# Four transformer blocks on one core: rows kept in expert order across two stages, raw context rows mixed ahead of their projection, rotation ahead of scaling

## What is computed

```
L0: m = memory @ W_mem.T                       # context projected to 256
    a = softmax(x @ m.T / 16);  c = a @ m
    x = rmsnorm(x + sigmoid([x, c] @ W_gate.T + b) * c)
L1, L3: vm = expert mask of the token          # two weight sets, v and l
    q, k, v = rope(where(vm, n(x) @ v_qkv, n(x) @ l_qkv))
    x += where(vm, ctx @ v_dense, ctx @ l_dense)      # causal self attention, 16 heads of 16
    x += cross_attention(n(x), context)               # 16 heads of 8
    x += where(vm, v_ffn(n(x)), l_ffn(n(x)))          # silu(gate) * up, 688 wide
L2: x += tanh(g) * latent_attention(layernorm(x), context)   # 16 heads of 64
    x += tanh(f) * gelu_ffn(layernorm(x))
```

## Time and profile before

| | us |
|---|---|
| median of 3 runs | 2231.86 |
| the profiled execution, its own time | 2225.6 |
| its span (first to last instruction) | 2223.8 |
| PE busy | 2066.6 (93%) |
| DVE busy | 1368.3 (62%) |
| ACT busy | 1139.9 (51%) |
| POOL busy | 853.1 (38%) |
| mean granted TensorE clock | 0.967 of full |

### The profile page before, as it was taken

One profiled execution on the slowest core, in us unless ns is written; L12 is line 12 of the kernel. 1 busy time (PEld: TensorE's weight loads), 2 busy tenths in 40 slices (PEclk: granted clock), 3 DMA queues, 4 the chain that ended last, 5 costly groups with the idle time before them and its releaser, 6 DMA issues.

```text
span 2223.8 us, 62412 instructions
## 1 busy us (share of the span) xinstructions
PE 2066.6 (93%) x23424; PEld 1669.0 (75%) x23425; DVE 1368.3 (62%) x2791; ACT 1139.9 (51%) x2603; POOL 853.1 (38%) x1109
## 2 busy tenths in 40 slices
PE   7988898879979998999999979999999979979998
PEld 5656676656659997788888868897777756659997
DVE  6776776757763333666666655554788867763343
ACT  4764555438853333445444534545566637863332
POOL 1655554438942221111111112222544428952222
PEclk9999999989989998999999999999999999989999
DMA  7426877734032112200000010002444424011111
GB/s 237 122 90 140 108 118 127 104 43 111 33 99 68 57 59 72 73 2 2 2 2 2 2 42 20 19 24 92 139 134 134 126 47 124 33 49 58 58 59 34
DMA packets 122751, 159.21 MB, mean 72 GB/s; under 512 B 40867, under 2 KB 99056, under 8 KB 122384
## 3 DMA queue, kind: packets, MB, share of 16 engines
q1 hardware_dynamic: 104720, 99.59, 15.6%
q0 software_dynamic: 16560, 55.23, 11.9%
q10 hardware_dynamic: 1232, 1.05, 0.2%
HBM read 86.69 MB, written 56.28 MB: 64 GB/s over the span
## 4 chain that ended last, share of the span: by engine, by line
PE 79%; DVE 7%; issue 3%; DMA 2%; ACT 1%; POOL 1%; another core or an unknown queue 0%; POOLq 0%; DVEq 0%; ACTq 0%; SPq 0%
PE ps_all L2477 4%; PE ps_all L2479 4%; PE ps_all L2478 4%; PE ps_all L1717 3%; PE ps_all L1689 3%; PE ps_all L1242 3%; PE ps_all L1228 3%; PE ps_all L1260 3%; PE ps_all L2051 2%; PE ps_all L2502 2%; PE ps_all L2504 2%; PE ps_all L2503 2%; PE ps_all L2487 2%; PE ps_all L1703 2%; PE ps_all L1676 2%
## 5 line engine op out<-in xcount | busy, mean ns | idle before, releaser
L410 POOL TENSOR_TENSOR a_probs<-a_probs,a_sm 128x1024 f32<-128x1024 f32 x32 | 60.9, 1903 | 346.8 <-DVE a_sm L405 346.8
L1436 POOL TENSOR_TENSOR pool_w<-s_qkt,const 128x512 f32<-128x512 f32 x128 | 131.4, 1048 | 105.6 <-ACT s_qkt L1364 98.3
L2477 PE MATMUL ps_all<-f_wh,f_xh 128*128 x396 | 153.7, 388 | 5.3 <-DVE f_xl L2623 5.3
L2183 ACT ACTIVATE self_w<-ps_all,a_q_bias 128x256 f32<-128x256 f32 x128 | 53.7, 471 | 184.7 <-PE ps_all L2027 184.7
L2479 PE MATMUL ps_all<-f_wl,f_xh 128*128 x396 | 148.0, 374 | 0.0
L2478 PE MATMUL ps_all<-f_wh,f_xl 128*128 x396 | 148.0, 374 | 0.0
L2618 DVE SCALAR_TENSOR_TENSOR f_h<-ps_all,rstd,f_act_g 128x688 f32<-128x688 f32 x66 | 61.7, 934 | 135.1 <-PE ps_all L2479 135.1
L1832 POOL TENSOR_TENSOR c_kx<-kv_k,const 128x512 f32<-128x512 f32 x128 | 131.3, 1051 | 3.9 <-PE ps_all L1689 2.3
L381 DVE TENSOR_REDUCE s_mx<-ps_all 128x8 f32<-128x512 f32 x128 | 82.5, 686 | 76.4 <-PE ps_all L1228 69.1
L2541 ACT ACTIVATE f_act_g<-ps_all,rstd 128x688 f32<-128x688 f32 x66 | 55.2, 837 | 134.7 <-PE ps_all L2479 134.7
L2502 PE MATMUL ps_all<-f_dh,f_hh 128*128 x396 | 118.3, 299 | 3.9 <-DVE f_hl L2633 3.9
(11 more groups left out here) (342 smaller groups left out, 6921.6 us busy)
## 6 DMA issues: line engine op xcount, KB each, us to landing
qkv_sorted<-pool_w SPq DMA_DIRECT2D x66, 392.0 KB, 4.3
pool_w<-pool_w SPq DMA_DIRECT2D x128, 68.0 KB
s_x_in<-x_sorted SPq DMA_DIRECT2D x66, 128.0 KB
f_x_in<-x_sorted SPq DMA_DIRECT2D x66, 128.0 KB, 2.0
x_res<-x_sorted SPq DMA_DIRECT2D x66, 128.0 KB, 2.1
x_sorted<-x_res POOLq DMA_DIRECT2D x1, 4224.0 KB, 17.3
l_rows<-in_x SPq DMA_DIRECT2D x32, 128.0 KB, 2.3
x_res<-in_x SPq DMA_DIRECT2D x32, 128.0 KB, 2.9
```

Source lines behind the costliest of these rows:

```text
L1436: ins = nc.gpsimd.tensor_tensor(kx[:, p % 2, c], qkt[:, p % 2, 2 + c].rearrange("p (b k) -> p b k", b=2).unsqueeze(2) .broadcast_to([P, 2, ...
L2477: nc.tensor.matmul(bank, x_high, wh[:, w_at], start=(c == 0), stop=False)
```

## The change

Five parts, which are one diff.

1. **Layer 0.** `memory` and its copy go. PE first multiplies raw context rows by the probabilities (`mix`, 128 columns), DVE copies the result to `mem_t`, and one step later `context` projects it to the 512 columns. `context_copy` goes too: `add_gated` reads the PSUM bank, the factor 0.5 moves into `w_both`, and the softmax's inverse sum into the last multiplication. Gate, addition and norm of a pair come one step later; the loops get one step more. Row buffers go from 4 to 6 and are freed by `mix`, not by `xt_`.
2. **Loads in layer 0.** Weights of self attention follow `load(13)`, the four mask loads follow `load(18)`, (20), (22) and (24), and the DVE step that makes masks moves from 9 to 25.
3. **Self attention (layers 1 and 3).** `rope_sum` stands ahead of `out_norm`, `qk_t` ahead of `out_t`, `qkt_copy` ahead of `out_high`. `put_home` goes.
4. **Gated stage of layer 1.** No `put_back`: SP writes each finished tile to `x_sorted` in sorted order (`kept_put`), four tiles behind its loads.
5. **Latent attention.** POOL gathers the pairs from `x_sorted`, two per group of two pairs, three groups ahead; `put_home` is done here, once per pair, and SP reads the home table at the end, behind the loads of the next weights.

```diff
-                R, X, M = 4, 3, 3
+                R, X = 6, 3
                     def load(p):
                         if p >= R:
-                            sp.wait_ge(xt_pe.handle, xt_pe.at(p - R + 1))
+                            sp.wait_ge(c_pe.handle, c_pe.at(p - R + 1))
...
-                    for p in range(2, 6):
-                        load(p)
-                    load_next(sp)
-                    load(6)
...
+                    for p in range(2, PAIRS):
                         load(p)
+                        if p == 13:
+                            load_next(sp)
+                        if p in (18, 20, 22, 24):
+                            load_mask((p - 18) // 2)
...
-                    def memory(p):
-
-                        if v_ok.due(p):
-                            pe.wait_ge(v_ok.handle, v_ok.at(p))
-                        nc.tensor.matmul(ps_d[:], xt[:, p % X, 2 * P:3 * P], w_both[:], start=True, stop=True) \
-                            .then_inc(v_pe.handle, 1)
+                    def mix(p):
+
+                        pe.wait_ge(pt_ok.handle, pt_ok.at(p + 1))
+                        if c_ok.due(p):
+                            pe.wait_ge(c_ok.handle, c_ok.at(p))
+                        nc.tensor.matmul(ps_d[:, 0:P], rows[:, p % R, D:D + DC], pt[:, p % 2], start=True, stop=True) \
+                            .then_inc(c_pe.handle, 1)
...
-                        nc.tensor.matmul(out_banks[p % 2][:], pt[:, p % 2], both[:, p % M], start=True, stop=True) \
+                        nc.tensor.matmul(out_banks[p % 2][:], mem_t[:, p % 2], w_both[:], start=True, stop=True) \
                             .then_inc(pv_pe.handle, 2)
...
-                        nc.vector.tensor_copy(both[:, p % M], ps_d[:]).then_inc(v_ok.handle, 1)
+                        nc.vector.tensor_copy(mem_t[:, p % 2], ps_d[:, 0:P]).then_inc(c_ok.handle, 1)
...
-                        nc.vector.scalar_tensor_tensor(gated[:], th[:, p % 2], 1.0, mc[:, p % 2], ALU.add, ALU.mult) \
-                            .then_inc(gated_ok.handle, 1)
+                        nc.vector.scalar_tensor_tensor(gated[:], th[:, p % 2], 1.0, out_banks[p % 2][:, 0:D],
+                                                       ALU.add, ALU.mult).then_inc(gated_ok.handle, 1)
                         dve.wait_ge(gated_ok.handle, gated_ok.at(p + 1))
-                        nc.vector.scalar_tensor_tensor(x_tile(p), gated[:], 0.5, x_tile(p), ALU.mult, ALU.add) \
+                        nc.vector.scalar_tensor_tensor(x_tile(p), gated[:], col(inv, p), x_tile(p), ALU.mult, ALU.add) \
...
                         if has(p + 2):
                             rope_products(p + 2)
+                            rope_sum(p + 2)
                         if has(p - 1):
                             out_norm(p - 1)
-                        if has(p + 2):
-                            rope_sum(p + 2)
...
-                        if n == 1:
-                            put_home(p)
...
+                    def put_sorted(t):
+                        sp.wait_ge(res_ok.handle, res_ok.at(t + 1))
+                        sp.dma_start(x_sorted[t * P:t * P + P, :], rows(t)).then_inc(kept_put.handle, 16)
...
+                    def gather(g):
+
+                        if xn_ok.due(2 * g - 6):
+                            pool.wait_ge(xn_ok.handle, xn_ok.at(2 * g - 6))
+                        for p in (2 * g, 2 * g + 1):
+                            pool.indirect_dma_start(x_tile(p), None, x_sorted,
+                                                    bass.IndirectOffsetOnAxis(slot_i[:, p:p + 1], 0)) \
+                                .then_inc(back_in[g % 4].handle, 16)
...
+                    pool.wait_ge(kept_put.handle, kept_put.at(NT))
+                    gather(0)
+                    gather(1)
                     rstd_(0)
+                    gather(2)
                     rstd_(1)
                     for p in range(PAIRS):
                         softmax_norm(pool, sm, probs, p, p % 2)
                         if p % 2 == 0 and has_group2(p // 2 + 2):
                             rstd_(p // 2 + 2)
+                        if p % 2 == 0 and has_group2(p // 2 + 3):
+                            gather(p // 2 + 3)
+                        put_home(p)
```

More of the change, by code:

```diff
@@ L268, in build @@
         back_put = count("back_put", 16)
-        back_in = [count(f"back_in{u}", 16) for u in range(2)]
+        kept_put = count("kept_put", 16)
+        back_in = [count(f"back_in{u}", 16) for u in range(4)]
         gu_pe = count("gu_pe", 2)
@@ L628, in _ @@
                     pe.wait_ge(wq_ok.handle, wq_ok.at(2))
-                    memory(0)
                     gate_x(0)
                     shapes_t()
-                    for p in range(PAIRS + 1):
+                    for p in range(PAIRS + 2):
                         if has(p):
@@ L638, in _ @@
                             query(p + 1)
-                            memory(p + 1)
                         if has(p + 2):
                             xt_(p + 2)
+                        if has(p - 2):
+                            context(p - 2)
                         if has(p + 1):
@@ L644, in _ @@
                         if has(p - 1):
-                            context(p - 1)
+                            mix(p - 1)
                         if p == 0:
@@ L988, in keep_context @@
                             .then_inc(ctx_ok.handle, 1)
-                    for p in range(PAIRS + 2):
+                    for p in range(PAIRS + 3):
                         if has(p):
@@ L1000, in _ @@
                             put_sorted(p - 4)
-                    for p in range(PAIRS - 2, PAIRS):
-                        put_sorted(p)
+                    put_sorted(PAIRS - 1)
                 loaded.base += 80
@@ L1651, in _ @@
                     load_next(sp)
-                    if n == 1:
-                        sp.wait_ge(home_put.handle, home_put.at(PAIRS))
-                        with nc.allow_non_contiguous_dma(reason="a table of words, once"):
-                            sp.dma_start(home_i[:], home_d.rearrange("(n p) a -> p (n a)", p=P)) \
-                                .then_inc(home_in.handle, 16)
                 @block.tensor
@@ L1996, in _ @@
                     previous_done(sp)
-                    sp.wait_ge(back_put.handle, back_put.at(0))
-                    back = x_back.rearrange("(n p) d -> p n d", p=P)
-                    for k, (lo, hi) in enumerate(((0, 4), (4, PAIRS))):
-                        sp.dma_start(x_res[:, lo * D:hi * D].rearrange("p (n d) -> p n d", d=D), back[:, lo:hi]) \
-                            .then_inc(back_in[k].handle, 16)
                     load_next(sp)
+                    sp.wait_ge(home_put.handle, home_put.at(PAIRS))
+                    with nc.allow_non_contiguous_dma(reason="a table of words, once"):
+                        sp.dma_start(home_i[:], home_d.rearrange("(n p) a -> p (n a)", p=P)) \
+                            .then_inc(home_in.handle, 16)
                 @block.tensor
@@ L2453, in _ @@
                             load_next(sp)
+                        if not store and t >= 4:
+                            put_sorted(t - 4)
                     if store:
                         sp.wait_ge(back_put.handle, back_put.at(NT))
+                    else:
+                        for t in range(NT - 4, NT):
+                            put_sorted(t)
                 @block.tensor
```

107 lines of the change are left out of this document (46 added, 61 removed).

## The result

| | median of the runs | range |
|---|---|---|
| before | 2230.32 us | 2225.55 to 2236.3 |
| after | 2176.66 us | 2165.11 to 2182.47 |
| ratio | 0.975 | 95% interval 0.9709 to 0.979 |

The profiled execution of after took 2182.47 us (span 2180.7), the longest of its four. Against the profiled execution of before, 2225.6 us, it is 43.1 us shorter; 57.7 were forecast. Terms of the sum missed it on both sides, and they partly cancel.

A forecast was written before the change was run, and what follows sets the result against it. It took PE to bound most stages, and DMA gathers behind four-byte scatters to slow self attention 1. Terms 39.2 + 8 + 10.5 = 57.7 us off the profiled 2225.6 gave 2168 us, range 2150 to 2192.

The forecast's parts named there:

- Table out of self attention 1: Self attention of layer 1: without `put_home` it runs like layer 3, 39.2 us less, bounds 20 and 41.
- Table in the latent stage: Latent stage: the moved scatters and new gathers on POOL are hidden by PE's work, cost 0.
- Start of the latent stage: Latent stage's start: plain write and two gathers replace scatter and load back; 0 taken, range -2 to +4 us.
- Rotation: Self attention, layers 1 and 3: rotation ahead of scaling removes 0.14 us idle per pair; -8 us, range -9 to +2.
- Layer 0: Layer 0: PE's step falls from 3.89 to 3.25 us, 20.5 us less; after delays elsewhere, -10.5 us.
- the two row loads: Layer 0: row loads issued nearer their use land late while `x_sorted` is zeroed; +2 us, range 0 to 10.
- POOL's two-scatter steps: Layer 0, steps 14 to 23: POOL is gapless and falls behind the shorter step; +3.5 us, between 0 and 6.3.
- the masks: Layer 0, DVE: the first steps' tables and the masks at step 25 have less room; together +3.5 us, 0 to 7.
- POOL's copy: Layer 0: with one two-input DVE instruction less, POOL's step might shrink to 3.64 us, returning 2.4 us; not counted.
- The slower one: Rival, latent stage: the scatter's cost moves along and holds up the gathers; for example 2248 us, chance 0.02.
- The case that half the excess stays: Rival, self attention 1: the scatter is not the whole cause and half the excess stays; 2188 us, chance 0.08.
- What was to show it: Signs: self attention 1 240 to 250 us, layer 0 step 3.25 us, no latent instruction waiting for a gather after the start.

The follow-up runs named there:

- e2: After, with the table's scatters of words back in the loop of self attention 1, at their old place ahead of the next gather: 2223.6 us, 0.9923 of before.
- e1: After once more, nothing edited, for a second profile: 2173.46 us, 0.9686 of before.
- e5: Before, with the 32 scatters of the table issued a second time in the latent stage, without row gathers there: 2260.04 us, 1.0078 of before.
- e12: After, with the table back in self attention 1 directly ahead of the next gather, but in rows of 512 bytes: 2164.43 us, 0.9717 of before.
- e9: After, with the table in rows of 512 bytes instead of words of four, scattered at the same place in the latent stage: 2169.58 us, 0.9673 of before.
- e3: After, with the 32 scatters moved from the latent stage into the gated stage of layer 1: 2174.5 us, 0.9687 of before.
- e8: After, with the next stage's weights in the latent stage loaded only when the first four row gathers have landed: 2168.81 us, 0.9662 of before.
- e4: After, with the rotation's sum, the rotated rows' transposes and their copy put back behind the scaling and its transposes: 2195.23 us, 0.9788 of before.
- e13: After, with the functions of layer 0 as they were in before: 2188.03 us, 0.9819 of before.
- e7: After, with layer 0's zeroing of the sorted rows cut into eleven pieces, one per step from the third on: 2175.64 us, 0.969 of before.
- e11: After, with e9's wide rows, e7, e8, and layer 0's next weights one transfer per tile from the fourteenth on: 2156.73 us, 0.9677 of before.
- e2b: After, with scatters of words back in self attention 1, but directly behind the gather of the same step: 2192.08 us, 0.9827 of before.

## Why the prediction was right, and where its terms were not

The largest term was right in place and mechanism, and so was the direction. That the total came within 9 us of the median is partly luck: against the profiled execution the forecast took off 14.6 us too much. The latent stage and its start (+13.6), layer 0 (+1.4) and the other stretches between stages (some +8) cost more than was allowed for, and the rotation gave 8 more than forecast. The range does not quite add up either: its lower end of 2150 is 4 us below what its own terms give (2158 - 2 - 2).

- **Table out of self attention 1, -39.2.** Right in place and mechanism, the bound of 41 too low: -39.7 remain of the stage's -47.6 when the rotation's 7.9 are taken off, 53 between e2 and e1. The price of one profile was taken as fixed, but it varies with the execution: over layer 3 of the same profile it is 39.2 us in before, 53 in e2 and 57 in e5. Late semaphore updates come with the words here too: 22 are 0.5 to 6 us late in before, none in after, in e12 or in before's layer 3.
- **Table in the latent stage, 0.** This step failed: 10.6 us in after, 15.8 in e1. I named PE's work as the cover, and it does cover POOL's time (e9) and the gathers (e2). What I left out is that a scatter of words delays more than its own queue. The profile of before had the warning: in self attention 1 the 16 engines were busy 73% of the time. Two delays come and go with the words in this stage: code fetches take 1.8 to 2.1 us instead of 1.1, and semaphore updates of the compute engines come late. The seven kernels here that scatter words in the latent stage have both (29 to 45 late updates, 406 to 412.6 us), the seven others have neither (395.1 to 396.9 us). The second delay is what the waits end with, and a third of the late updates in after have no fetch under way. That the engines wait for code, as the expectations of e2, e3, e5 and e9 have it, is thus not shown. Why the updates come late is open.
- **Start of the latent stage, 0 in -2 to +4.** +3.0. Inside the range; the reason that I named for its upper end, weights competing with the gathers, is what happened (e8).
- **Rotation, -8.** Mis-sized by half: 16.5 (e4), 0.35 per pair instead of 0.14. The idle time of the earlier trace rows is not the price of a stall. PE's timeline in self attention 3, before:

```profile
1639.29 0.28 PE L1184 MATMUL ps_all<-s_wh,s_xl 128*128 x1
1639.41 0.38 PE L1267 MATMUL ps_all<-const,s_on 128*128 128x128 f32 x2
1639.93 0.66 PE L1210 MATMUL ps_all<-const,s_roped 128*128 128x128 f32 x4
1640.52 0.41 PE L1220 MATMUL ps_all<-causal_b,ident_b 64*64 64x512 bf16 x4
```

and after:

```profile
1601.19 0.28 PE L1173 MATMUL ps_all<-s_wh,s_xl 128*128 x1
1601.31 0.60 PE L1199 MATMUL ps_all<-const,s_roped 128*128 128x128 f32 x4
1601.74 0.38 PE L1256 MATMUL ps_all<-const,s_on 128*128 128x128 f32 x2
1602.06 0.41 PE L1209 MATMUL ps_all<-causal_b,ident_b 64*64 64x512 bf16 x4
```

  From the first row's start to the last row's: 1.23 us before, 0.87 after. Gapless matmuls begin here some 0.16 us ahead of the end of the one before, by the ends that the profile models; a stall loses this overlap too, and it shows as longer "busy" time.
- **Layer 0, -10.5.** -9.1 (-9.5 by e13), with other terms than forecast. PE's step is 3.25 us as forecast, some 19.7 us in 31 steps. Of these 13.4 are lost, where I had 10: the two row loads cost 9.1 us instead of 2 (steps of 9.56 and 6.05 us against 3.25), POOL's two-scatter steps 2.3 instead of 3.5 (late in only four steps, by 0.57 each), the masks 2.1 (a step of 5.38) and the tables about 0.6, together 2.7 instead of 3.5. These make 14.1, of which 0.7 come back in shorter steps, so the tail cost nothing where I had 1. And the first gated addition comes at 27.4 us instead of 30.3, a gain that no term had.
- **POOL's copy.** Timeline of POOL in after:

```profile
94.59 1.24 POOL L971 DMA_INDIRECT x_sorted<-x_res,slot_i  x1 [0.19 <-issue]
96.14 0.97 POOL L971 DMA_INDIRECT x_sorted<-x_res,slot_i  x1 [0.30 <-issue]
97.11 0.30 POOL L977 COPY ctx_all<-l_xt 128x128 f32<-128x128 f32 x1
```

  The copy fell from 0.55 to 0.30 us, but the first scatter's issue rose from 1.04 to 1.24: 3.81 us per step instead of 3.88. The Trainium skill, "GPSIMD Engine Reference", section 8 (Key points), on interfaces shared with VectorE, would have had 3.64; the copy agrees with it, the step does not.
- **The rivals.** The slower one had the right place, the scatter's cost moving along to the latent stage, but the wrong victim: no instruction waits for a gather there after the start. The case that half the excess stays is out.
- **What was to show it.** Layer 1 as even as layer 3, gather under 4.5 us, step of 3.25 us: seen. The idle time ahead of the rotated rows' transposes is gone but for three of the last steps, 2.04 us each. "No instruction waits for a gather" came true and was too narrow a sign, as the latent stage lost its time elsewhere.

## What to carry to other kernels

Price a scatter of four-byte words by what else goes on while it lands, other queues' transfers and the engines' semaphores included, and not by its own 1 us of issue; moving it to a stage with idle queues was not free, since PE had no idle time there. Write such a table in rows of 512 bytes instead (e9, e12). Price a stall of PE by the distance between starts with and without it; its idle time was less than half of it here. A delay behind a burst of transfers moved to the next burst when one was cut, and went when both were (e7 against e11; cutting the weights alone was not run).

## What the runs showed of the hardware that was not expected

- Words of four bytes slow the packets of other transfers: POOL's queue needs 43.9% of the engines' time for 11.05 MB with them and 17.7% for 12.87 MB with rows of 512 bytes, and in e2b SP's queue pays. The Trainium skill, "DMA: Bandwidth & Descriptors", section Specifications, states a read-modify-write below 512 bytes; the runs agree with that bound at the two sizes tried, but show neither the mechanism nor where between 4 and 512 bytes it begins.
- With such words around, semaphore updates of PE, DVE and ACT come 0.5 to 4.3 us behind the end of their instructions (latent stage of after, e1, e4, e5); without them no update of the latent stage is more than 0.5 us late (before, e2, e3, e9, e12).
- The stretch from self attention 1 to cross attention 1, in which the change touches little (the table's reading is gone), takes 16.6 us (e1), 18.5 (before) or 22.2 (after), and goes with the granted clock. Windows of after at that place:

```profile
433.00:440.00 7.00, 4.91 (x23) 3.10 (x22) 3.30 (x6) 2.34 (x9) 4.81 (x6) 0.50 0.48 76
...
446.00:452.00 6.00, 6.00 (x61) 3.90 (x57) 2.65 (x7) 3.36 (x8) 2.39 (x3) 0.50 1.07 220
...
456.00:470.00 14.00, 14.00 (x229) 9.63 (x229) 10.65 (x24) 10.85 (x30) 10.78 (x13) 1.00 0.45 156
```

  PE has idle time at the start of the stage, and the clock stays at 0.50 (1.2 GHz) for some 20 us; before had 0.50 in the first 7 us of the same stretch, 0.78 and 0.85 in the next 12, and then 1.00. Why it differs between executions is open; it makes up to 5.6 us of a single profile's total.
